# Selective scan beside a feed-forward layer: a quarter of the scan's input reaches the state partitions by DMA in fp32 instead of through TensorE and ScalarE

## The chip, the cores and the metric

The kernel runs on one core of one Trainium2 chip. The metric is the time of one execution on the device in microseconds (us), the median of several runs. TensorE multiplies matrices into PSUM, VectorE and ScalarE work elementwise on SBUF and PSUM, GpSimd works elementwise on SBUF alone, and SyncE issues the DMAs. In the profile they are PE (PEld is its weight load), DVE, ACT, POOL and SP (SPq for what SyncE's queue issues and waits for).

## The reference

Four sublayers follow each other over 2048 tokens of 512 features: linear attention, a feed-forward layer with a Hadamard transform, a selective scan, and a second feed-forward layer. After each comes a residual and a layer norm. The scan is what the change touches:

```python
x = _layernorm(x + _L0_attn_ref(x, ...), axis=-1)
x = _layernorm(x + _L0_ffn_ref(x, ...), axis=-1)
x = _layernorm(x + _L1_attn_ref(x, ...), axis=-1)      # the selective scan
x = _layernorm(x + _L1_ffn_ref(x, ...), axis=-1)

def step(h, inp):                                      # 512 tokens, 4 sequences
    delta_t, B_t, C_t, u_t = inp
    dA = jnp.exp(delta_t[:, :, None] * A[None])
    dBu = (delta_t * u_t)[:, :, None] * B_t[:, None, :]
    h = dA * h + dBu
    y_t = jnp.einsum('bdn,bn->bd', h, C_t)
    return (h, y_t)
```

Each of the 512 features has 32 states. delta is a softplus of a low-rank product of x, and u is x.

## The kernel before

The attention comes first, in a phase of its own. The rest is one phase, `trunk_phase`, in which both feed-forward layers and the scan overlap. Features lie on the partitions, tokens on the free axis, in four tiles of 512 tokens.

The order is written out by hand. Each engine's program is a loop over the same ticks, from -24 to 795, and in each tick each engine adds the instructions that its own conditions name. Engines run freely and meet at semaphores alone. Each tick from 0 to about 770 holds six matmuls of a feed-forward layer (two groups of `three_passes`, L84 to L86; gate, up, and down into the PSUM bank `y_or_aux`). VectorE takes what they give: `silu` (L1524), `hidden` (L1530), and `add` (L1536), which adds the down product to x. The same bank `y_or_aux` serves the sums of the layer norms and the products that prepare the scan, in turns counted by `s_bank`.

Scan step s runs in tick 134 + s, for s from 0 to 511. A step treats 4 features with 32 states each, which fill 128 partitions, over the 512 tokens of a tile. Four steps are a quad; the fourth step of a quad (j = 3, `BY_POOL`) has its product with B made by GpSimd. Eight quads (32 steps) are 128 features, numbered o from 0 to 15. A step is made so:

- SyncE loads delta, spread over the state partitions by a broadcast from DRAM, two steps per DMA, into a ring of six (`delta_load`, L1108), six steps ahead.
- ScalarE makes the decay, exp(delta times A), into one of two PSUM slots (`decay`, L1439).
- TensorE spreads delta*x over the state partitions. Its input are three bf16 parts of delta*x, stacked on 96 partitions (`stk`, loaded by `stack_load`, L1099). The matmul `spread_input` (L1288) picks 4 features and writes one of two PSUM slots `uu`.
- VectorE multiplies that slot with B (`inject`, L1566) one tick ahead of the scan of three steps in four. For the fourth, ScalarE copies the slot to SBUF (`copy_input`, L1447, into the single buffer `us`), since GpSimd reads no PSUM here, and GpSimd multiplies (`inject`, L1673, into `dp`).
- VectorE runs the scan instruction itself (`scan`, L1586).
- GpSimd multiplies the states with C (`times_c`, L1682), and once per quad TensorE sums over the states into `scan_y` (`sum_states`, L1297), five ticks later.
- Once every 32 steps VectorE adds the finished sum to x (`leave`, L1595), and the next `scan_y` waits for that.

The slots `uu` are taken in the order that `spread_turn` gives. GpSimd's share is spread two quads early, in the third tick of a quad, between the shares of VectorE. With two slots, each spread waits for the release of the spread two turns before. The shares of VectorE are released by `inject`, the share of GpSimd by ScalarE's copy.

For each o, delta and delta*x are made two to eight ticks apart (`step_size` L1553, `step_input` L1557), delta*x is cut into its three parts by ScalarE and GpSimd, and SyncE stores both to DRAM (`delta_store` L1086, `parts_store` L1091).

## Time and profile before

| what | value |
|---|---|
| median of 3 runs | 2034.74 us (2029.73 to 2044.35) |
| the profiled execution: its time | 2037.56 us |
| its span in the profile | 2035.8 us |
| the scan, from the first scan instruction to the last | 598.6 to 1827.9 us |
| busy over the span: PE / DVE / ACT / POOL | 1820.4 / 1443.7 / 951.8 / 1285.2 us |
| DMA moved | 427.37 MB |

The span runs from the first to the last instruction of the profiled execution; its time is 1.8 us longer. A row of the profile names the line of the kernel, the engine, the operation, and output<-inputs. A number in brackets with an arrow is the time for which the engine stood idle just before, and what ended it. Matmul records overlap: one matmul's row lasts 0.39 us, while the next starts 0.23 us after it. "PEclk" is the share of full speed that TensorE's clock was granted.

### The profile page before, as it was taken

The numbers are of one execution on the slowest core, as the hardware profiler recorded it, in microseconds if no ns is written. First come the engines' busy times: TensorE is split into PE (matmuls) and PEld (weight loads), VectorE is DVE, ScalarE is ACT, GpSimd is POOL, SyncE is SP. The second block draws the span as 40 slices with busy tenths as digits, with TensorE's granted clock in tenths as the row PEclk, the third lists the DMA queues.
The fourth block names the chain that finished last, engine by engine and source line by source line (L and its number), as shares of the span: only waits on it lengthen the run. The fifth ranks groups of instructions, "written<-read, shape, count | busy, mean of one in ns | idle before, by whom it ended". The sixth has DMA issues, their size and how long they took to land. (4 is left out here: it accounts for less than half of the span.)

```text
span 2035.8 us, 27701 instructions
## 1 busy us (share of the span) xinstructions
PE 1820.4 (89%) x9552; PEld 1144.8 (56%) x9552; DVE 1443.7 (71%) x1825; ACT 951.8 (47%) x1591; POOL 1285.2 (63%) x987
## 2 busy tenths in 40 slices
PE   7899897799998999988998898988988898899997
PEld 5566665568655554544554454554554555567784
DVE  3533424243339998898998999799998999993433
ACT  5434252443255555655555455645554545443212
POOL 4444431366129987897877897697977887782110
PEclk9999999999999999999999999999999999999999
DMA  6433322769558875786776775486766676764451
GB/s 227 141 114 115 115 69 72 264 219 333 193 183 290 280 272 204 250 278 209 251 250 204 257 254 215 177 271 214 263 221 229 219 254 208 256 223 170 186 188 61
DMA packets 132925, 427.37 MB, mean 210 GB/s; under 512 B 29200, under 2 KB 35984, under 8 KB 116016
## 3 DMA queue, kind: packets, MB, share of 16 engines
q1 hardware_dynamic: 132784, 425.59, 60.1%
q8 instruction: 76, 1.25, 0.2%
q14 instruction: 65, 0.53, 0.1%
HBM read 356.34 MB, written 69.21 MB: 209 GB/s over the span
## 5 line engine op out<-in xcount | busy, mean ns | idle before, releaser
L1682 POOL TENSOR_TENSOR h_times_c<-h_states,c_rep 128x512 f32<-128x512 f32 x512 | 671.4, 1323 | 197.7 <-PE scan_y L1297 134.1
L1439 ACT ACTIVATE decay<-delta_on_states,a_neg 128x512 f32<-128x512 f32 x512 | 354.3, 693 | 481.5 <-DVE h_states L1586 469.4
L1648 POOL TENSOR_TENSOR h_lo<-silu_in_h_lo,h_hi 128x512 fp32r<-128x512 f32 x128 | 168.1, 1313 | 250.0 <-ACT h_hi L1354 249.3
L1536 DVE TENSOR_TENSOR x<-x,y_or_aux 128x512 f32<-128x512 f32 x256 | 173.8, 679 | 212.8 <-PE y_or_aux L86 212.8
L1288 PE MATMUL du_spread<-stack,selectors 96*128 96x512 bf16 x512 | 201.2, 393 | 95.6 <-DVE d_b L1566 75.5
L1566 DVE TENSOR_TENSOR d_b<-du_spread,b_rep 128x512 f32<-128x512 f32 x384 | 255.3, 665 | 3.6 <-PE du_spread L1288 3.6
L84 PE MATMUL y_or_aux<-h_hi,w 128*128 128x512 f32 x512 | 239.5, 468 | 15.9 <-ACT b_rep L1404 6.6
L1586 DVE TENSOR_TENSOR_SCAN h_states<-decay,h_last,d_b 128x512 f32<-128x512 f32 x192 | 245.2, 1277 | 9.2 <-ACT decay L1439 4.9
L84 PE MATMUL gate<-x_hi,w 128*128 128x512 f32 x512 | 243.7, 476 | 7.4 <-DVE w L1519 7.1
L84 PE MATMUL up<-x_hi,w 128*128 128x512 f32 x512 | 246.4, 481 | 0.0
L1586 DVE TENSOR_TENSOR_SCAN h_states<-decay,d_b 128x512 f32<-128x512 f32 x192 | 233.6, 1217 | 13.8 <-ACT decay L1439 9.6
L85 PE MATMUL gate<-x_lo,w 128*128 128x512 f32 x512 | 203.2, 397 | 0.0
L85 PE MATMUL up<-x_lo,w 128*128 128x512 f32 x512 | 202.6, 396 | 0.0
L86 PE MATMUL gate<-x_hi,w 128*128 128x512 f32 x512 | 202.5, 395 | 0.0
L86 PE MATMUL up<-x_hi,w 128*128 128x512 f32 x512 | 201.9, 394 | 0.0
L85 PE MATMUL y_or_aux<-h_lo,w 128*128 128x512 f32 x512 | 201.7, 394 | 0.0
L86 PE MATMUL y_or_aux<-h_hi,w 128*128 128x512 f32 x512 | 201.1, 393 | 0.0
L1288 PEld LDWEIGHTS du_spread<-stack,selectors 96*128 96x128 bf16 x512 | 49.5, 97 | 256.4 <-DVE d_b L1566 130.5
L1673 POOL TENSOR_TENSOR d_b_by_pool<-du_copied,b_rep 128x512 f32<-128x512 f32 x128 | 169.6, 1325 | 1.7 <-ACT du_copied L1447 1.7
L1354 ACT CAST h_hi<-silu_in_h_lo 128x512 fp32r<-128x512 f32 x128 | 78.9, 616 | 171.6 <-DVE silu_in_h_lo L1530 171.4
L1530 DVE SCALAR_TENSOR_TENSOR silu_in_h_lo<-silu_in_h_lo,up 128x512 f32<-128x512 f32 x128 | 86.8, 678 | 96.2 <-PE up L86 96.0
L1297 PE MATMUL scan_y<-h_times_c,sum_selectors 128*32 128x512 f32 x1024 | 141.0, 623 | 13.2 <-DVE x L1595 12.8
(167 smaller groups left out, 3142.5 us busy)
## 6 DMA issues: line engine op xcount, KB each, us to landing
delta_on_states<-delta SPq DMA_DIRECT2D x256, 512.0 KB, 5.2
w<-w_split SPq DMA_DIRECT2D x112, 1024.0 KB, 6.7
w<-w_split SPq DMA_DIRECT2D x112, 512.0 KB, 6.3
w_split<-w_presplit_hi_lo SPq DMA_DIRECT2D x32, 512.0 KB, 3.7
w_split<-w SPq DMA_DIRECT2D x16, 1024.0 KB, 6.6
w_presplit_hi_lo<-in_w13b SPq DMA_DIRECT2D x32, 256.0 KB, 3.9
h_times_c<-in_w13a SPq DMA_DIRECT2D x16, 512.0 KB, 4.6
w_split<-w SPq DMA_DIRECT2D x16, 512.0 KB, 6.7
```

What stands on the lines that cost most here:

```text
L84: pe.matmul(out, w_hi, x_hi, start=first, stop=False)
L85: pe.matmul(out, w_hi, x_lo, start=False, stop=False)
L86: return pe.matmul(out, w_lo, x_hi, start=False, stop=last)
L1288: pe.matmul(uu[:, i % NU], sel[:, r, :], stk[:, o % 2, j]).then_inc(s_uu, 1)
L1297: mm = pe.matmul(yb[j * 32:(j + 1) * 32, :], ysel[:, r, :], hc[:, (s + j) % NC_], start=(r == 0), stop=(r == QB - 1), skip_group_check=Tru ...
L1439: act.activation(da[:, s % ND], dring[:, s % NR], ACT.Exp, scale=a[:, column(s):column(s) + 1]).then_inc(s_da, 1)
L1536: dve.tensor_tensor(xt, xt, bank[:, :], ALU.add).then_inc(s_bank, 1)
L1566: dve.tensor_tensor(db[:, by_dve(s) % NB], uu[:, i % NU], brep[:, tile_of(s // SPO) % 2], ALU.mult).then_inc(s_db, 1)
L1586: dve.tensor_tensor_scan(hs[:, s % NH], da[:, s % ND], data, initial, ALU.mult, ALU.add).then_inc(s_hs, 1)
L1648: pool.tensor_tensor(hl[:, idx % 4], sg[:, idx % 4], hh[:, idx % 4].bitcast(F32), ALU.subtract).then_inc(s_hl, 1)
L1673: pool.tensor_tensor(dp[:, quad % 2], us[:, :], brep[:, tile_of(JB * quad // SPO) % 2], ALU.mult).then_inc(s_dp, 1)
L1682: pool.tensor_tensor(hc[:, s % NC_], hs[:, s % NH], crep[:, tile_of(s // SPO) % 2], ALU.mult).then_inc(s_hc, 1)
```

## The change

GpSimd's quarter of delta*x is the last 32 of the 128 features of each o. They leave the path of parts, stack, spread and copy. `delta_x_store` stores them in fp32 to the DRAM tensor `delta_x`, and `delta_x_load` reads them back with a broadcast over the state partitions, one DMA of 256 KB for each quad, into a ring of three (`pring`), from which GpSimd multiplies. The parts shrink from 128 to 96 features. The spreads that are left are numbered by `by_dve`, so that each now waits for VectorE's product two turns before, among the turns of VectorE alone. In other respects the program's order is kept. A buffer of the second layer's weight splitting shrinks from three slots to two, which makes room in SBUF; its instructions stay the same.

```diff
+PD = 32 * BY_POOL
-def spread_turn(s):
-    quad, j = divmod(s, JB)
-    if j == BY_POOL:
-        return JB * quad - 3 if quad else 0
-    return JB * quad + 2 + j - (quad == STEPS // JB - 1)
...
-    parts_d = nc.dram_tensor("delta_x_parts", (NO, P, 3, TT), BF16, kind="Internal").ap()
+    parts_d = nc.dram_tensor("delta_x_parts", (NO, PD, 3, TT), BF16, kind="Internal").ap()
+    du_d = nc.dram_tensor("delta_x", (NO, QD, QB, TT), F32, kind="Internal").ap()
...
-        us = p.sb("du_copied", [P, TT])
+        pring = p.sb("delta_x_on_states", [P, NP, TT])
...
+                def delta_x_store(t, m):
+                    n = KD * t + m
+                    sp.wait_ge(s_du, n + 1)
+                    if n:
+                        sp.wait_ge(s_dx, 16 * n)
+                    sp.dma_start(du_d[n].rearrange("d r t -> r d t"), soft_of(t)[PD:P, m]).then_inc(s_dx, 16)
+
+                def delta_x_load(quad):
+                    o, r = divmod(quad, QB)
+                    if r == 0 or quad < NP:
+                        sp.wait_ge(s_dx, 16 * (o + 1))
+                    if quad >= NP:
+                        sp.wait_ge(s_dp, quad - NP + 1)
+                    sp.dma_start(pring[:, quad % NP], du_d[o, :, r].unsqueeze(0).to_broadcast([NS, QD, TT]))\
+                      .then_inc(s_pr[quad % NP], 16)
...
                     if tick - 2 in PARTS_AT:
                         delta_store(*PARTS_AT[tick - 2])
+                        delta_x_store(*PARTS_AT[tick - 2])
...
+                        for quad in range(NP):
+                            delta_x_load(quad)
+                    if s >= 0 and s % JB == 2 and s // JB + NP + 1 < STEPS // JB:
+                        if s == 2:
+                            delta_x_load(NP)
+                        delta_x_load(s // JB + NP + 1)
...
                 def spread_input(s):
                     o, r, j = place(s)
-                    i = spread_turn(s)
...
-                        if turn == BY_POOL and quad + 3 > STEPS // JB:
-                            pe.wait_ge(s_db, by_dve(JB * quad + JB) + 1)
-                        elif turn == BY_POOL:
-                            pe.wait_ge(s_us, quad + 3)
-                        else:
-                            pe.wait_ge(s_db, by_dve(JB * quad + turn) + 1)
+                    i = by_dve(s)
+                    if i >= NU:
+                        pe.wait_ge(s_db, i - NU + 1)
                     pe.matmul(uu[:, i % NU], sel[:, r, :], stk[:, o % 2, j]).then_inc(s_uu, 1)
...
-                    if s == -1:
-                        spread_input(BY_POOL)
-                        spread_input(JB + BY_POOL)
...
-                    if 0 <= s and s % JB == 2 and s + 2 * JB + 1 < STEPS:
-                        spread_input(s + 2 * JB + 1)
...
-                def copy_input(quad):
-                    i = spread_turn(JB * quad + BY_POOL)
-                    act.wait_ge(s_uu, i + 1)
-                    if quad:
-                        act.wait_ge(s_dp, quad)
-                    act.copy(us[:, :], uu[:, i % NU]).then_inc(s_us, 1)
...
                 def inject(quad):
-                    pool.wait_ge(s_us, quad + 1)
+                    pool.wait_ge(s_pr[quad % NP], 16 * (quad // NP + 1))
...
-                    pool.tensor_tensor(dp[:, quad % 2], us[:, :], brep[:, tile_of(JB * quad // SPO) % 2],
+                    pool.tensor_tensor(dp[:, quad % 2], pring[:, quad % NP], brep[:, tile_of(JB * quad // SPO) % 2],
                                        ALU.mult).then_inc(s_dp, 1)
```

The first place is on TensorE in the quad that ends the 128 features o = 3, near the 908th microsecond of the profile. Before, GpSimd's spread stands between two pieces of the feed-forward layer's up product:

```order
L85 MATMUL up<-x_lo,w 128x512
L86 MATMUL up<-x_hi,w 128x512
L1288 MATMUL du_spread<-stack,selectors 128x512 [waits scan_db]
L84 MATMUL up<-x_hi,w 128x512
L85 MATMUL up<-x_lo,w 128x512
L86 MATMUL up<-x_hi,w 128x512
```

In the changed kernel the two pieces follow each other:

```order
L85 MATMUL up<-x_lo,w 128x512
L86 MATMUL up<-x_hi,w 128x512
L84 MATMUL up<-x_hi,w 128x512
L85 MATMUL up<-x_lo,w 128x512
L86 MATMUL up<-x_hi,w 128x512
```

One spread with its wait went out of each quad, and twelve matmuls of the layer now stand between the spread ahead of this place and the one behind it. The second place is on TensorE a little further on, up to the sum over states that waits for VectorE's `leave` (scan_yout). Before, the last spread ahead of it waits for ScalarE's copy:

```order
L86 MATMUL y_or_aux<-h_hi,w 128x512
L1288 MATMUL du_spread<-stack,selectors 128x512 [waits scan_du_copied]
L84 MATMUL gate<-x_hi,w 128x512 [waits silu_done,w13_in0]
L85 MATMUL gate<-x_lo,w 128x512
L86 MATMUL gate<-x_hi,w 128x512
L1297 MATMUL scan_y<-h_times_c,sum_selectors 32x512 [waits scan_yout,scan_hc]
```

In the changed kernel that wait is for VectorE's product (scan_db):

```order
L86 MATMUL y_or_aux<-h_hi,w 128x512
L1296 MATMUL du_spread<-stack,selectors 128x512 [waits scan_db]
L84 MATMUL gate<-x_hi,w 128x512 [waits silu_done,w13_in0]
L85 MATMUL gate<-x_lo,w 128x512
L86 MATMUL gate<-x_hi,w 128x512
L1305 MATMUL scan_y<-h_times_c,sum_selectors 32x512 [waits scan_yout,scan_hc]
```

Nothing moved here but the wait: the two slots are now turned by VectorE alone. The third place is SyncE's queue at the last store of delta for the second tile, near 905 us. Before:

```order
L1086 DMA delta<-delta_in_x_lo 4x32x512 [waits prep_delta]
L1108 DMA delta_on_states<-delta 128x1x1024 [waits scan_decay] x3
L1065 DMA w<-w_split 128x2048 [waits up_done]
L1091 DMA delta_x_parts<-delta_x_parts_out 128x1536 [waits prep_low]
L1108 DMA delta_on_states<-delta 128x1x1024 [waits scan_decay,delta_stored]
```

In the changed kernel:

```order
L1081 DMA delta<-delta_in_x_lo 4x32x512 [waits prep_delta]
L1088 DMA delta_x<-soft_in_x_hi 8x4x512 [waits delta_x_stored,prep_du]
L1119 DMA delta_on_states<-delta 128x1x1024 [waits scan_decay] x2
L1096 DMA delta_x_on_states<-delta_x 128x1x512 [waits scan_db_by_pool]
L1119 DMA delta_on_states<-delta 128x1x1024 [waits scan_decay]
L1060 DMA w<-w_split 128x2048 [waits up_done]
```

A store that waits for delta*x now stands ahead of the next load of delta, and in every quad a load that waits for GpSimd's product.

## Rows read from the trace of the kernel before

**Rows 1.** Windows: busy us (instructions) of PE, PEld, DVE, ACT, POOL; PEclk, DMA share, GB/s.

```profile
598.60:1827.90 1229.30, 1099.66 (x4829) 627.80 (x4828) 1144.49 (x1346) 656.30 (x1135) 1005.26 (x783) 0.98 0.69 239
```

**Rows 2.** Waits of DVE, 598.6 to 1827.9: us in total, times, longest.

```profile
DVE x L1536 <- PE y_or_aux L86: 33.6, 25, 4.0
DVE silu_in_h_lo L1530 <- PE up L86: 26.5, 19, 5.0
DVE h_states L1586 <- ACT decay L1439: 16.0, 9, 4.2
DVE d_b L1566 <- PE du_spread L1288: 1.4, 2, 1.0
```

**Rows 3.** Waits of PE and ACT in the same stretch.

```profile
PE du_spread L1288 <- DVE d_b L1566: 75.5, 99, 3.0
PE du_spread L1288 <- ACT du_copied L1447: 17.4, 13, 3.6
...
ACT decay L1439 <- DVE h_states L1586: 469.4, 404, 5.2
ACT decay L1439 <- DMA delta_on_states<-delta: 11.4, 5, 4.4
```

**Rows 4.** Timeline of PE and DVE around 917 us (start, duration).

```profile
908.12 0.39 PE L1288 MATMUL du_spread<-stack,selectors 96*128 96x512 bf16 x1 [0.23 <-DVE d_b L1566]
...
912.44 0.39 PE L1288 MATMUL du_spread<-stack,selectors 96*128 96x512 bf16 x1 [0.62 <-DVE d_b L1566]
...
913.83 0.39 PE L86 MATMUL y_or_aux<-h_hi,w 128*128 128x512 f32 x1
914.06 0.39 PE L1288 MATMUL du_spread<-stack,selectors 96*128 96x512 bf16 x1
...
914.53 0.40 PE L85 MATMUL gate<-x_lo,w 128*128 128x512 f32 x1
914.76 0.40 PE L86 MATMUL gate<-x_hi,w 128*128 128x512 f32 x1
...
917.04 0.74 DVE L1595 SCALAR_TENSOR_TENSOR x<-x,scan_feat,scan_y 128x512 f32<-128x512 f32 x1
...
917.93 1.93 PE L1297 MATMUL scan_y<-h_times_c,sum_selectors 128*32 128x512 f32 x8 [2.77 <-DVE x L1595]
```

**Rows 5.** Windows of the tile du_spread: PE, PEld, DVE, ACT busy us (instructions).

```profile
793.00:836.00 43.00, 6.26 (x16) 1.55 (x16) 8.65 (x13) 2.37 (x4) 1.00 0.62 223
1045.00:1080.00 35.00, 5.08 (x13) 1.26 (x13) 7.31 (x11) 1.76 (x3) 1.00 0.60 210
1271.00:1316.00 45.00, 6.25 (x16) 1.55 (x16) 8.65 (x13) 2.37 (x4) 0.96 0.51 188
```

**Rows 6.** Timeline of PE and DVE, 1726 to 1734 us.

```profile
1727.30 0.39 PE L1288 MATMUL du_spread<-stack,selectors 96*128 96x512 bf16 x1 [0.60 <-DVE d_b L1566]
...
1733.44 0.69 DVE L1536 TENSOR_TENSOR x<-x,y_or_aux 128x512 f32<-128x512 f32 x1 [0.69 <-PE y_or_aux L86]
```

**Rows 7.** Timeline of ACT after a softplus (1082 to 1091 us).

```profile
1088.51 0.58 ACT L1447 COPY du_copied<-du_spread 128x512 f32<-128x512 f32 x1
1088.99 0.70 ACT L1439 ACTIVATE decay<-delta_on_states,a_neg 128x512 f32<-128x512 f32 x1
```

**Rows 8.** Timeline at the scan's start (592 to 600 us).

```profile
595.39 0.58 ACT L1447 COPY du_copied<-du_spread 128x512 f32<-128x512 f32 x1 [1.62 <-PE du_spread L1288]
...
597.89 0.70 ACT L1439 ACTIVATE decay<-delta_on_states,a_neg 128x512 f32<-128x512 f32 x1
```

**Rows 9.** Windows of the eleven stretches at half clock within the scan.

```profile
917.30:923.90 6.60, 5.97 (x21) 1.62 (x22) 5.42 (x6) 0.77 (x2) 4.53 (x5) 0.50 0.79 268
...
1777.50:1780.70 3.20, 3.12 (x11) 1.06 (x11) 1.71 (x2) 0.69 (x1) 1.02 (x1) 0.50 0.50 164
sum 45.40, PE 41.38 PEld 19.16 DVE 28.46 ACT 16.87 POOL 22.78; mean PE 3.76 PEld 1.74 DVE 2.59 ACT 1.53 POOL 2.07
```

**Rows 10.** Timeline of PE, 1600 to 1611 us.

```profile
1600.31 0.39 PE L1288 MATMUL du_spread<-stack,selectors 96*128 96x512 bf16 x1 [0.97 <-DVE d_b L1566]
...
1606.51 0.39 PE L1288 MATMUL du_spread<-stack,selectors 96*128 96x512 bf16 x1 [1.59 <-DVE d_b L1566]
```

**Rows 11.** The tile delta_on_states, and SyncE's waits, 598.6 to 1827.9.

```profile
DMA to landing us min/median/max: 3.7/5.2/11.5
...
SPq L1086 <- DVE delta_in_x_lo L1553: 36.1, 13, 4.4
```

56 lines of the change are left out of this document (24 added, 32 removed).

## The prediction

> **What bounds the kernel now.** I read the windows first, by stage. The change acts in the scan alone, 598.6 to 1827.9 us. There DVE is busy 1144 of 1229 us, 93%, and PE 1100 us, 89% [rows 1]. So the two are nearly level, and the order of instructions couples them tick by tick. The waits tell which one sets the pace. DVE, asked whom it waits for, names little: 61.5 us for PE in 46 waits (33.6 + 26.5 + 1.4), and 16.0 us for ACT's decay [rows 2]. PE waits for DVE's products 99 times, 75.5 us, and for ACT's copy of GpSimd's share 13 times, 17.4 us [rows 3]. DVE is thus the bound over most of the scan, and PE becomes it in places. DVE's work is not touched. Whatever PE, ACT or DMA gain can shorten the scan by 61.5 + 16.0 = 77.5 us at most, all DVE idleness there. ACT is far from the bound: of 511 decays 404 wait for the scan before [rows 3].
>
> **The change part by part.**
>
> *One spread fewer per quad on PE, 128 in all.* Its record says 0.39 us, but records overlap; what counts is the distance of starts. With a spread between, L86 to L85 two matmuls on is 913.83 to 914.53, 0.70 us; two ordinary steps are 2 x 0.23 (914.53 to 914.76) [rows 4]. So a spread costs 0.24 us, and 128 of them 31 us of PE work. Most lies where PE would only wait for DVE instead. It counts where DVE waits for PE. I followed PE back from each of DVE's waits to its last idle time over 0.33 us. Three long stretches of unbroken PE work (793 to 836, 1045 to 1080, 1271 to 1316 us) hold 17.9 of the 61.5 us, and 4 + 3 + 4 = 11 spreads for GpSimd, which ACT's count of copies shows [rows 5]: 11 x 0.24 = 2.6 us. The other 30 or so waits end runs of 2 to 15 us, less than two quads, with between none and one such spread each: 0 to 7 us. I counted 13, so 3 us. Together **5.6 us**, with 2.6 and 10 as ends.
>
> *Looser waits of the spreads that stay.* Before, four spreads per quad turned two slots; a spread waited for the product made two ticks before. Now three turn them: the spread for a quad's last step of VectorE still waits for a product of two ticks before, the other two for one of three ticks before. At 912.44 PE idled 0.62 us for a product that it will no longer need [rows 4]. PE gets further ahead, and this is worth something where a short wait of DVE follows closely: 0.69 us at 1733.44 after 0.60 us at 1727.30 [rows 6]. Ten DVE waits of 0.3 to 0.9 us have such a predecessor within 7 us, 5.5 us together. I take **5 us**, ends 0 and 12 (twice as many, if longer waits shrink too).
>
> *128 copies less on ACT.* 0.58 us each, 74 us, hidden under ACT's waiting for the scan [rows 3]. Where the softplus has blocked ACT, the copy stands ahead of the decay that DVE waits for: 1088.51 before 1088.99 [rows 7], 0.5 us, at up to three tiles. At the start of the scan the first decay waits for two copies and a product by GpSimd between them: from 595.39 to 597.89, 2.5 us [rows 8]; about 2 of them fall away, since DVE's first product needs PE's spread, which also comes earlier. Sum **3 us**, ends 1 and 4.
>
> *DMA.* 128 loads of 256 KB are 33.6 MB. The scan's share of 0.69 at 239 GB/s [rows 1] means 346 GB/s when all queues work: 0.76 us a load, 97 us in all, 8 points more of share. Parts and stack shrink by 3 MB, the new stores add 1. Loads of delta land in 5.2 us at the median and 11.5 at worst [rows 11], six steps ahead, and a decay waited for one only five times, 11.4 us [rows 3]. Two things delay them. SyncE's queue is in order: the store of delta*x waits for a product that VectorE makes one tick after the one that the store of delta waits for (already 36.1 us at 13 stores [rows 11]), so the load behind comes some 2.4 us later, 12 times within the scan. And each quad's new load waits for GpSimd's product two quads on; behind it stand the next loads of delta and of weights. In the timeline that product ends ahead of the next delta load's issue in all but 9 of 123 quads. ACT's decays have slack: they wait 1.2 us on average for DVE (469.4 / 404). I take **3 us of loss**, with 0 and 12.
>
> *Clock.* Within the scan the clock was granted at 0.50, the 1.2 GHz level, in eleven stretches, 917.3 the first [rows 9]. DVE was busy in 28.46 of their 45.4 us, so it lost 16.9 us, 1.5 per stretch. The stretch at 917 stands right behind an idle PE: 2.77 us before the sum that waits for VectorE's `leave` [rows 4]. The change makes this idle time longer. From the spread at 908.12 PE needs 0.24 + 12 x 0.23 us to the next spread, 0.24 + 6 x 0.23 to the one after, and 0.24 + 3 x 0.23 to the sum; no product that these wait for comes too late, so it is there at 913.7. Its last matmul ends some 0.2 us later, and it idles until 917.93: 4.0 us against 2.77. Elsewhere waits of one quad that stood apart come together at the one tight spread: 0.97 us at 1600.31 and 1.59 at 1606.51 [rows 10] become 2.56 us in one place. I take four more half-clock stretches at 1.5 us: **6 us of loss**, ends 0 (where the clock falls while PE is ahead, DVE loses nothing) and 20. The Trainium skill, TensorE: Matmul & The Clock Gate, "Why this matters for your kernels", warns against idle gaps between bursts of matmuls, since the clock then falls back to half rate. The trace agrees at 917 us; by that rule this change, which does nothing for PE but make it idle, could give back its gain.
>
> *Nothing else.* GpSimd's product reads SBUF as before; its operand is loaded ten ticks ahead, against 5.2 us for a landing, so that load hides. Were it late, GpSimd and the scan of that step would stand. The parts are cut on 96 instead of 128 partitions; whether that takes three quarters of the time or all of it, it is work of ACT and POOL off the path, and the term is nothing.
>
> Sum: -5.6 - 5 - 3 + 3 + 6 = -4.6 us on the profiled execution's 2037.56, that is 2033.0. That execution is 2.8 us above the median, so the forecast for the median is **2030 us**, 4.6 below 2034.74. With the ends that help, -10 - 12 - 4, it is 2009; with those that hurt, -2.6 - 0 - 1 + 12 + 20, it is 2063.
>
> **The rivals.**
>
> *PE's 31 us come through whole.* If DVE and PE take turns so closely that every delay of PE is passed on, the whole saving counts, 2035 - 31 = 2004, perhaps less the copies that PE waited for. For it: PE is busy 89% of the scan, and VectorE's 77.5 us of waits could hold the gain. Against it: PE had 75.5 us of waiting for DVE left in the same stretch, and the stretches in which DVE waits hold some two dozen of the 128 spreads.
>
> *The slower clock.* Where PE's idle time comes together in one place of each quad, the clock falls far more often. At 1.5 us a stretch, 7 more than before use up what the other terms leave (13.6 - 3 = 10.6 us), and 21 more make the kernel 1% slower, (10.6 + 20.3) / 1.5. If one quad in four brings one, 32 more: 2034.7 + 48 - 10.6, 2072 us. For it: [rows 4, 9, 10]. Against it: nearly all of PE's single waits are below the 2.77 us seen at 917, and with longer lead DVE is covered while PE is slow.
>
> *Loads of delta come late.* The place is SyncE's queue, the price what a late decay costs. The margin: a load needs 5.2 us and has about six steps, some 14 us, less SyncE's own wait. It decides when a landing passes the need, as happened five times. If every eighth of the 256 loads came late by 1.2 us beyond ACT's slack, that is 38 us: 2034.7 - 13.6 + 6 + 38, 2065. For it: landings of up to 11.5 us already and DMA share near 0.8 in some slices, to which 8 points are added. Against it: only 11.4 us of such waits in 511 decays, most of them absorbed by ACT.
>
> **How the numbers follow.** The forecast's own case, a small change with a range of 2018 to 2045, has 0.66; the saving in full 0.14; the clock 0.09; the late loads 0.11. The range from 2009 to 2055 leaves out the whole-saving case's lower half and the far ends of the two slow ones, together below 2 in 10. A measurement of this kernel can tell about 1%, 20 us, from no change (its own runs differ by 15). Faster by more than that: most of the full-saving case and the best end of the forecast's, 0.16. Slower by more: most of both slow cases, 0.15. Within: 0.69.
>
> **What would show it.** In the profile after: DVE still busy about 1144 us in the scan and its waits for PE near 50 us instead of 61.5; PE's busy time down by some 30 us, and its waits for DVE's products up by about as much, in fewer and longer pieces; no wait for a copy; ACT's busy time down by 74 us; DMA bytes up to 459 MB and the scan's share near 0.76; decay waits for DMA from 11 to perhaps 20 us; 13 to 17 stretches at half clock. I would be wrong if DVE's waits for PE fell by half, if PE's clock was granted below 0.96 in the scan, or if decays waited for DMA by more than 30 us.

## The result: slower by 0.7%

The changed kernel takes 2048.73 us (median of 8 runs, 2043.82 to 2054.36), the kernel before on the same chip 2035.57. The ratio is 1.0068, 95% interval 1.0045 to 1.0091. Forecast were 2030 us and a range of 2009 to 2055: the time lies in the range, the sign is wrong. The profiled execution took 2043.82 us (span 2042.0); its scan runs from 593.6 to 1834.2 us, 1240.6 us against 1229.3.

Its window answers to [rows 1] (busy us and instructions of PE, PEld, DVE, ACT, POOL; PEclk, DMA share, GB/s):

```profile
593.60:1834.20 1240.60, 1093.17 (x4707) 639.98 (x4707) 1153.27 (x1346) 592.78 (x1009) 1005.50 (x784) 0.96 0.76 263
```

DVE is busy 8.8 us longer with the same 1346 instructions. ACT lost 64 us, the DMA share is 0.76 as forecast. PE has 122 records fewer but only 6.5 us less busy time: the clock is 0.96 instead of 0.98. The waits of DVE, PE, ACT and SyncE in that stretch answer to [rows 2, 3, 11]:

```profile
DVE x L1529 <- PE y_or_aux L86: 36.9, 26, 3.8
DVE silu_in_h_lo L1523 <- PE up L86: 23.9, 16, 5.2
DVE h_states L1579 <- ACT decay L1444: 15.4, 9, 3.7
DVE d_b L1559 <- PE du_spread L1296: 1.7, 4, 0.8
...
PE du_spread L1296 <- DVE d_b L1559: 73.3, 51, 5.3
...
ACT decay L1444 <- DVE h_states L1579: 497.0, 377, 5.4
ACT decay L1444 <- DMA delta_on_states<-delta: 71.1, 29, 5.1
...
SPq L1096 <- POOL d_b_by_pool L1666: 214.8, 78, 6.5
...
SPq L1088 <- DVE soft_in_x_hi L1550: 30.2, 14, 4.4
```

Three things are to be seen. DVE waits for PE 62.5 us, 61.5 before: no gain from PE's relief shows there. PE's waits for products are half as many (51 for 99) and as long in sum. And ACT's decay waits for a load of delta 29 times, 71.1 us, where it was 5 times and 11.4 us.

Where DVE's 8.8 us are shows when its groups are laid side by side (line, shapes, count | busy us, mean ns | idle before). The kernel before:

```profile
L1542 DVE TENSOR_TENSOR x<-x,mean_or_rank 128x512 f32<-128x512 f32 x32 | 36.5, 1145 | 0.0
L1548 DVE TENSOR_TENSOR x<-x,rstd 128x512 f32<-128x512 f32 x32 | 32.8, 1032 | 0.0
L1553 DVE TENSOR_TENSOR delta_in_x_lo<-delta_in_x_lo,soft_in_x_hi 128x512 f32<-128x512 f32 x15 | 23.2, 1546 | 0.0
L1557 DVE TENSOR_TENSOR soft_in_x_hi<-delta_in_x_lo,x 128x512 f32<-128x512 f32 x15 | 15.2, 1014 | 0.0
```

The changed kernel:

```profile
L1535 DVE TENSOR_TENSOR x<-x,mean_or_rank 128x512 f32<-128x512 f32 x32 | 36.5, 1147 | 0.0
L1541 DVE TENSOR_TENSOR x<-x,rstd 128x512 f32<-128x512 f32 x32 | 34.9, 1095 | 0.0
L1546 DVE TENSOR_TENSOR delta_in_x_lo<-delta_in_x_lo,soft_in_x_hi 128x512 f32<-128x512 f32 x15 | 27.8, 1854 | 0.0
L1550 DVE TENSOR_TENSOR soft_in_x_hi<-delta_in_x_lo,x 128x512 f32<-128x512 f32 x15 | 17.2, 1144 | 0.0
```

These 94 are the only DVE instructions of the scan with both operands in SBUF. Where GpSimd isn't working they last 0.68 us, like their neighbours; beside GpSimd's back-to-back products up to 4.0 in the changed kernel, 4.1 in the kernel before and 4.9 in other kernels of the study. The waiting lies inside the recorded duration, so it counts as busy time and stands in no view of waits. I call **excess** their sum less 94 x 0.685 us: 43.7 before, 52.3 after (over the single records; the rows give it within 0.4). Here is one, in the changed kernel, first DVE's row, then GpSimd's:

```profile
627.33 2.03 DVE L1546 TENSOR_TENSOR delta_in_x_lo<-delta_in_x_lo,soft_in_x_hi 128x512 f32<-128x512 f32 x1
...
626.27 1.30 POOL L1666 TENSOR_TENSOR d_b_by_pool<-delta_x_on_states,b_rep 128x512 f32<-128x512 f32 x1
627.52 2.97 POOL L1675 TENSOR_TENSOR h_times_c<-h_states,c_rep 128x512 f32<-128x512 f32 x2
```

and the same instruction before:

```profile
632.48 0.78 DVE L1553 TENSOR_TENSOR delta_in_x_lo<-delta_in_x_lo,soft_in_x_hi 128x512 f32<-128x512 f32 x1
...
631.41 1.29 POOL L1673 TENSOR_TENSOR d_b_by_pool<-du_copied,b_rep 128x512 f32<-128x512 f32 x1
632.65 2.99 POOL L1682 TENSOR_TENSOR h_times_c<-h_states,c_rep 128x512 f32<-128x512 f32 x2
```

All stand in the same order, alike to 0.04 us. GpSimd's first product ends 0.23 us after DVE's instruction starts. Before, DVE gets its turn then; after, GpSimd's next product does, and DVE waits another 1.25 us. The Trainium skill, SBUF — State Buffer, "SBUF: two separate sides", says of the read and write port that the two engines share that whichever instruction starts first holds it for its whole length and the other blocks. The trace agrees, and shows more: DVE can lose several turns in a row (4.9 us is the end of the running product, three whole ones, and its own time).

The half-clock stretches of the scan, 24 instead of eleven, answer to [rows 9]; two of them and the sum:

```profile
872.30:879.10 6.80, 5.94 (x15) 4.31 (x15) 6.80 (x10) 3.44 (x7) 6.50 (x6) 0.50 0.84 270
...
1554.90:1561.80 6.90, 6.29 (x21) 2.11 (x22) 2.24 (x3) 1.18 (x2) 0.73 (x1) 0.51 0.25 78
...
sum 106.30, PE 97.69 PEld 58.44 DVE 88.46 ACT 49.31 POOL 71.97; mean PE 4.07 PEld 2.43 DVE 3.69 ACT 2.05 POOL 3.00
```

In many DVE stays busy throughout (6.80 of 6.80 us at 872), in some it starves. In all it was idle 106.3 - 88.5 = 17.8 us, against 16.9 in [rows 9]: twice the stretches, and as much idle time of DVE inside them. What PE's slower work costs DVE after a stretch has ended is not in that sum.

### The profile page after: what moved, and what is told of

Its sections match the earlier page's. It is cut to its first block and busy times, and to the rows that moved or that the text cites. A ratio compares the mean times of both kernels' runs of the same rounds, so it can differ in the third digit from the quotient of the medians.

```text
span 2042.0 us, 27348 instructions
## 1 busy us (share of the span) xinstructions
PE 1811.8 (89%) x9424; PEld 1155.3 (57%) x9424; DVE 1452.2 (71%) x1825; ACT 887.0 (43%) x1463; POOL 1283.8 (63%) x987
## 5 line engine op out<-in xcount | busy, mean ns | idle before, releaser
L84 PE MATMUL up<-x_hi,w 128*128 128x512 f32 x512 | 241.5, 472 | 0.0
L1296 PE MATMUL du_spread<-stack,selectors 96*128 96x512 bf16 x384 | 153.6, 400 | 74.4 <-DVE d_b L1559 73.3
L85 PE MATMUL y_or_aux<-h_lo,w 128*128 128x512 f32 x512 | 205.9, 402 | 0.0
L86 PE MATMUL up<-x_hi,w 128*128 128x512 f32 x512 | 202.3, 395 | 0.0
L1666 POOL TENSOR_TENSOR d_b_by_pool<-delta_x_on_states,b_rep 128x512 f32<-128x512 f32 x128 | 171.0, 1336 | 4.3 <-DMA delta_x_on_states<-delta_x 4.3
L84 PEld LDWEIGHTS y_or_aux<-h_hi,w 128*128 128x128 f32 x512 | 100.0, 195 | 96.1 <-issue 29.3
L84 PEld LDWEIGHTS gate<-x_hi,w 128*128 128x128 f32 x512 | 101.7, 199 | 90.5 <-issue 68.8
```

The lines of the kernel that those rows point to most:

```text
L84: pe.matmul(out, w_hi, x_hi, start=first, stop=False)
L85: pe.matmul(out, w_hi, x_lo, start=False, stop=False)
L86: return pe.matmul(out, w_lo, x_hi, start=False, stop=last)
L1296: pe.matmul(uu[:, i % NU], sel[:, r, :], stk[:, o % 2, j]).then_inc(s_uu, 1)
L1666: pool.tensor_tensor(dp[:, quad % 2], pring[:, quad % NP], brep[:, tile_of(JB * quad // SPO) % 2], ALU.mult).then_inc(s_dp, 1)
```

## The experiments

All 18 experiments were timed against the kernel before on the same chip; short_before and short_after, which do less work, are given in the text below. In this table, ratio is to that kernel with its 95% interval, excess, DVE's idle time (gaps over 0.15 us) and half-clock stretches are of the profiled scan, and "late" is what decays waited for loads of delta (us, times).

| kernel | median us | ratio | excess | idle | stretches | late |
|---|---|---|---|---|---|---|
| before | 2034.74 | 1 | 43.7 | 76.2 | 11 | 11.4, 5 |
| before_again | 2033.77 | 0.9999 [0.9984, 1.0015] | 47.4 | 75.1 | 14 | 11.6, 5 |
| null_before | 2034.31 | 0.9996 [0.9981, 1.0012] | 41.6 | 75.6 | 12 | 11.3, 5 |
| before_moved | 2033.27 | 0.9996 [0.9979, 1.0013] | 46.3 | 68.4 | 10 | 16.6, 8 |
| dma96_before | 2034.99 | 0.9999 [0.9981, 1.0018] | 45.2 | 72.9 | 13 | 3.2, 2 |
| before_plus_stores | 2035.94 | 1.0005 [0.9985, 1.0025] | 37.9 | 72.9 | 11 | 16.5, 10 |
| parts96_before | 2039.80 | 1.0030 [1.0015, 1.0045] | 49.4 | 69.0 | 13 | 5.9, 4 |
| before_plus_loads | 2039.72 | 1.0046 [1.0024, 1.0068] | 41.6 | 78.8 | 11 | 74.9, 30 |
| fed_by_dma | 2051.60 | 1.0074 [1.0046, 1.0101] | 54.1 | 77.3 | 13 | 59.7, 25 |
| no_copy | 2049.93 | 1.0057 [1.0037, 1.0078] | 60.9 | 76.7 | 15 | 70.2, 27 |
| tight_waits | 2052.37 | 1.0084 [1.0059, 1.0109] | 58.5 | 77.6 | 17 | 77.8, 27 |
| the change | 2048.73 | 1.0068 [1.0045, 1.0091] | 52.3 | 78.2 | 24 | 71.1, 29 |
| after_moved | 2052.55 | 1.0083 [1.0062, 1.0105] | 54.7 | 83.9 | 30 | 73.9, 27 |
| no_loads | 2046.51 | 1.0071 [1.0051, 1.0091] | 57.0 | 79.1 | 26 | 20.4, 9 |
| double_spread | 2054.41 | 1.0104 [1.0079, 1.0129] | 51.7 | 90.0 | 26 | 82.9, 29 |
| yield_before | 2020.61 | 0.9922 [0.9908, 0.9937] | 25.1 | 80.6 | 12 | 9.8, 6 |
| yield_fed | 2031.42 | 0.9978 [0.9961, 0.9994] | 24.8 | 85.1 | 11 | 52.0, 28 |
| yield_after | 2034.26 | 0.9987 [0.9972, 1.0002] | 26.2 | 94.7 | 24 | 110.7, 41 |

In all of these the scan's length less excess less idle is 1109.0 to 1110.5 us. The rest, DVE's own work, is the same everywhere, so a longer scan shows as one of the two. This is bookkeeping, not a cause: one cause can appear as either. And a profile is one execution only: before_plus_loads was profiled in one of 2037.79 us, beside 2037.56 for the kernel before, and its scan there is 1.4 us longer, though its median is 0.46% above. The ratios carry the argument; the profiles show where to look.

### First: clock, DMA or the looser waits?

**tight_waits**, the changed kernel with two waits as tight as before.

```diff
-                        pe.wait_ge(s_db, i - NU + 1)
+                        pe.wait_ge(s_db, i if s % JB == 0 else i - NU + 1)
...
                         spread_input(s + 1)
+                    if 0 <= s < STEPS and s % JB == 2:
+                        pe.wait_ge(s_db, by_dve(s - 1) + 1)
```

> The changed kernel with the waits of before put back on TensorE, without the matmul and the copy: the first spread of a quad waits for VectorE's product of two ticks before instead of three, and in the third tick of each quad TensorE waits for the product that GpSimd's spread used to wait for. Nothing else is altered. Theory clock (the looser waits gather TensorE's idle time into single long pieces, after which its clock falls to half): the 24 stretches at half clock within the scan fall to 14 or fewer and the time from 2049 to 2035 to 2041 us. Theory DMA (the new loads and their place in SyncE's queue cost the time): 2047 to 2051 us, whatever the clock does. Theory lead (the forecast's term, looser waits are worth 5 us): 2052 to 2056 us.

**no_loads**, the changed kernel without 125 of the 128 loads; GpSimd multiplies the first three rows of delta*x again and again.

```diff
-                    if s >= 0 and s % JB == 2 and s // JB + NP + 1 < STEPS // JB:
-                        ...
-                        delta_x_load(s // JB + NP + 1)
...
-                    pool.wait_ge(s_pr[quad % NP], 16 * (quad // NP + 1))
+                    pool.wait_ge(s_pr[quad % NP], 16)
```

> The changed kernel with the three first loads of delta*x onto the states alone; the other 125 loads of 256 KB and their waits on SyncE are left out, and GpSimd multiplies what stands in its three buffers, so that its quarter of the scan is computed from wrong input. Theory DMA: the time falls from 2049 to 2034 to 2040 us, decays wait for DMA as before the change (11 us). Theory clock: it stays at 2045 to 2050 us with 20 or more stretches at half clock within the scan.

**before_plus_loads**, the kernel before with the change's stores and 124 loads of the same size and place, used by nobody. They all land in one buffer, and to make room for it the edit also takes over the change's smaller buffer of weight splitting, which the expectation doesn't mention:

```diff
-        pre = p.sb("w_presplit", [P, 3, TT])
+        pre = p.sb("w_presplit", [P, 2, TT])
+        spare = p.sb("delta_x_on_states", [P, TT])
...
+                        delta_x_store(*PARTS_AT[tick - 2])
...
+                    if s >= 0 and s % JB == 2 and s // JB + 4 < STEPS // JB:
+                        delta_x_load(s // JB + 4)
```

> The kernel before with the change's DMA traffic added and nothing taken away: one store of 64 KB beside each store of delta, with the wait for delta*x, and one broadcast load of 256 KB per quad (124 in all) at the change's place in SyncE's queue with its wait for GpSimd's product. Nobody reads what is loaded; the store takes delta instead of delta*x. Theory DMA: the time rises from 2036 to 2046 to 2052 us. Theory clock: it stays at 2035 to 2040 us with 9 to 14 stretches at half clock, since TensorE's waits are those of before.

**double_spread**, the changed kernel with each quad's third spread done twice.

```diff
+                    if j == BY_POOL - 1:
+                        pe.matmul(uu[:, i % NU], sel[:, r, :], stk[:, o % 2, j])
                     pe.matmul(uu[:, i % NU], sel[:, r, :], stk[:, o % 2, j]).then_inc(s_uu, 1)
```

> The changed kernel with the third spread of each quad issued twice into the same slot, so that TensorE has as many spreads as before the change (512) and keeps the looser waits; this prices the 31 us of work that the change takes from TensorE. If the forecast's term is right (5.6 us of the 31 count), 2052 to 2057 us against 2049. If TensorE's work counts in full, 2075 to 2080 us. Theory clock: the doubled matmul fills 0.24 us of each quad's idle time, so that some stretches at half clock go and the time may stay at 2047 to 2051 us.

Traffic and smaller buffer together cost the kernel before 0.46%. What the traffic does shows in the waits of ACT and SyncE in before_plus_loads:

```profile
ACT decay L1463 <- DMA delta_on_states<-delta: 74.9, 30, 5.2
...
SPq L1127 <- ACT decay L1463: 371.2, 170, 9.6
SPq L1105 <- POOL d_b_by_pool L1697: 163.9, 71, 5.5
```

and the landings of delta's loads there:

```profile
DMA to landing us min/median/max: 3.6/6.3/13.4
```

SyncE used to stand where it waits for ACT's decay (682.4 us in the kernel before) and issued the load of delta as soon as a buffer was free. Now it stands 71 times behind GpSimd's product first, and the load lands in 6.3 instead of 5.2 us. DVE's waits for the decay are 20.8 us there, 16.0 before, so late decays account for about 5 us in that profile. But no_loads is no faster than the change, though its decays wait only 20.4 us: in the changed kernel the loads cost -0.03%, give or take 0.30. Tight waits give nothing back: waits and clock together (17 half-clock stretches instead of 24) are worth 0.16%, give or take 0.34. The second spread costs 0.36%, give or take 0.34; it brings idle time (90.0), not clock stretches.

### Second: feed, copy, or contended instructions?

**fed_by_dma**, the changed kernel with the fourth spread and ACT's copy of it in their old order and with their old waits, both unread (the ring of loads has two buffers instead of three). **no_copy**, the same without the copy and its waits.

```diff
+                    if 0 <= s and s % JB == 2 and s + 2 * JB + 1 < STEPS:
+                        spread_input(s + 2 * JB + 1)
...
+                    if 0 <= s < STEPS and s % JB == BY_POOL and s // JB + 2 < STEPS // JB:
+                        copy_input(s // JB + 2)
...
                     pool.wait_ge(s_pr[quad % NP], 16 * (quad // NP + 1))
+                    pool.wait_ge(s_us, quad + 1)
```

> The changed kernel with TensorE's fourth spread of each quad and ScalarE's copy of it put back, in the order and with the waits of before; nobody uses the copy, GpSimd multiplies the loaded delta*x (two buffers instead of three) but still waits for the copy as before. It separates GpSimd's feed from what TensorE and ScalarE no longer do. Contention theory (VectorE's 94 instructions with both operands in SBUF wait for GpSimd's, and GpSimd stands in another phase to them once the copy and the spread are gone): as before_plus_loads, 2036 to 2042, ratio 1.000 to 1.004, the excess of the 94 at 40 to 46 us. Clock theory (TensorE's gathered idle time): the idle is not gathered, 11 to 13 half-clock stretches, same time. DMA theory: 2040 to 2046, since all DMA of the change is here. Feed theory (that GpSimd reads another buffer is itself the cause): 2045 to 2050 and an excess above 50 us.

> The changed kernel with TensorE's fourth spread put back (its result unread) but without ScalarE's copy; the spread that follows it in its slot waits for nobody. Beside the run with the copy it shows what the copy's going does, beside the one with before's tight waits and three spreads what the spread's going does. Contention theory: the excess of the 94 instructions jumps where the coupling of GpSimd to the copy goes, so 50 to 58 us here, 2044 to 2051. Clock theory: with the fourth spread TensorE idles less, 11 to 15 stretches and 2036 to 2041. DMA theory: as fed_by_dma. If neither spread nor copy matters by itself the excess is 43 to 50 and the time 2038 to 2044.

This turned the study. With all of PE's and ACT's work back the kernel is as slow as the change, 1.0074, at 13 stretches. From there to the change (no_copy, tight_waits, the change) the ratio moves by -0.17, +0.27 and -0.16%, together -0.06%: what PE and ACT save, less what the clock takes, is nothing within 0.4%. The loss was there before.

That difference of two terms need not be made of two zeros. no_copy and double_spread both have four spreads in each quad, no copy, and the same loads; double_spread has the looser waits and 26 half-clock stretches for 15, and it is 0.47% slower, give or take 0.32 (they differ besides in a buffer of the ring and in the place of the fourth spread). The single executions point the same way. The kernel before was run 29 times on one chip: its mean granted clock went from 0.975 to 0.987, and each 0.001 less goes with 1.3 us more (1.3 to 1.6 on four chips). In the changed kernel, whose median clock is 0.965 for the 0.979 to 0.980 of the kernel before, it is 1.2 us over eight executions. This is a correlation, over whole executions and not the scan alone. So a clock that takes some 10 us and a relief of PE that gives them back are as possible as two terms near nothing; no run separates them.

**short_before** and **short_after**: the 94 instructions, and those of the norms outside the scan, on one column (most of the norms and of delta is left out).

```diff
-                    dve.tensor_tensor(xt, xt, rstd[:, :], ALU.mult).then_inc(s_x, 1)
+                    dve.tensor_tensor(xt[:, :1], xt[:, :1], rstd[:, :1], ALU.mult).then_inc(s_x, 1)
```

> The kernel before, in which VectorE's instructions with both operands in SBUF (step size, step input, and the two of each norm) work on one column instead of 512, everything else in place: most of the norms and of delta and delta*x is left out, so the output is another one. It takes the contended instructions away. By 94 x 0.68 + 43.7 us of excess, less what TensorE then bounds, the scan gets 60 to 105 us shorter, and the norms outside it too: 1880 to 1960 us. What counts is its distance to the same edit of the changed kernel.

> The changed kernel with the same edit (VectorE's instructions with both operands in SBUF work on one column; most of the norms and of delta and delta*x is left out). Contention theory: with the contended instructions gone, so is the loss: short_after minus short_before is between -12 and +4 us, instead of +13. Clock theory: the loss stays or grows, since a less busy VectorE leaves TensorE the bound: +8 to +20. DMA theory: +5 to +13.

They took 1971.98 (ratio 0.9676, 0.9648 to 0.9704) and 1987.98 us (0.9758, 0.9731 to 0.9786): 16 us apart, which only the range given for the clock holds. The edit did not take the contention away, though: one column lasts 0.16 us where GpSimd isn't in the way, and 0.60 and 0.69 us on average (step 303: 0.47 in the one, 1.71 in the other), so these instructions wait for their turn whatever their length. In the profiles the two scans are 19.9 us apart (1180.6 and 1200.5), of which 12.0 are idle time and 8.4 these instructions. So the runs say little on contention, and they don't decide for the clock either.

### Third: does chance decide, and can the contention be removed?

**before_again** is the kernel before. **null_before** has a wait more on GpSimd that never holds.

```diff
                 def inject(quad):
+                    pool.wait_ge(s_lo13, 1)
                     pool.wait_ge(s_us, quad + 1)
```

> The kernel before, unchanged. It shows how much the time, VectorE's waits and the excess of its 94 instructions with both operands in SBUF vary without any edit. Theory that the arbitration between VectorE and GpSimd falls out the same way in each execution of one program: ratio 1.000 within 0.002, excess 42 to 46 us, the same instructions long (step 14 at 0.78 us, 303 at 0.97, 319 at 1.05). If it falls out anew each time: excess 44 to 60 us, other instructions long.

> The kernel before with one wait more on GpSimd ahead of each quad's product, on a semaphore that was reached long before: nothing waits for anything new, only GpSimd's instruction stream is longer by 128 entries. Theory of chance (any edit of GpSimd's stream redraws the arbitration, and the kernel before has a good draw): excess 48 to 60 us and 2040 to 2050 us, as with the change, without any part of the change. Theory that the change's own parts (feed, DMA, clock) cost the time: as the kernel before, 2031 to 2039 us, excess 42 to 46.

My theory that any edit redraws the turns, and that the kernel before has a good draw, fell: both times are the same within 0.16%. Single turns do fall differently (step 319: 1.05, 0.86, 2.33 us; step 122 in the unchanged kernel 1.67 and 2.91), with 41.6 to 47.4 us in sum. A difference of excess of some 4 us between two profiles thus can't be told from chance.

**yield_before** and **yield_after**: GpSimd waits until DVE has done its contended instruction of the tick.

```diff
                     if 0 <= s - 1 < STEPS:
+                        if tick in PARTS_AT:
+                            t, m = PARTS_AT[tick]
+                            pool.wait_ge(s_de, KD * t + m + 1)
+                        ...            (s_du at tick - 1, s_c and s_x of the norms likewise)
                         times_c(s - 1)
```

> The kernel before, in which GpSimd waits, before its product with C in those ticks of the scan where VectorE has an instruction with both operands in SBUF, until that instruction is done. GpSimd can then be at most one instruction ahead in the way. Contention theory: the excess falls from 43.7 us to 10 to 30, and the scan shortens by a half or all of that, 2005 to 2030 us; if GpSimd's own waits come back to VectorE through its products (up to 0.7 us at each), as much is lost: 2035 to 2050.

> The changed kernel with the same waits of GpSimd for VectorE's contended instructions. Contention theory: the excess comes to the same 10 to 30 us as in the kernel before with these waits, and the two times to within 6 us of each other instead of 13, at 2008 to 2035. If the loss of the change lies elsewhere (DMA, clock, waits for TensorE) the two stay 10 to 16 us apart.

Both gain 0.8% (0.9922; 0.9987 / 1.0068 = 0.992), and yield_before at 2020.61 us is the fastest kernel here that does all the work. Its groups:

```profile
L1548 DVE TENSOR_TENSOR x<-x,rstd 128x512 f32<-128x512 f32 x32 | 30.1, 945 | 0.0
L1542 DVE TENSOR_TENSOR x<-x,mean_or_rank 128x512 f32<-128x512 f32 x32 | 28.1, 882 | 0.0
L1553 DVE TENSOR_TENSOR delta_in_x_lo<-delta_in_x_lo,soft_in_x_hi 128x512 f32<-128x512 f32 x15 | 18.2, 1216 | 0.0
L1557 DVE TENSOR_TENSOR soft_in_x_hi<-delta_in_x_lo,x 128x512 f32<-128x512 f32 x15 | 12.8, 854 | 0.0
```

Excess 25.1 instead of 43.7, 18.6 us, of which 4.4 come back as idle time and 13.3 shorten the scan (1216.0). But the two stay 14 us apart at the same excess. The difference stands in idle time now, 94.7 against 80.6. So contention is a cost of both kernels, not the cause of their difference.

### Fourth: addresses, cut parts, and which part of them

**before_moved** and **after_moved** exchange two SBUF tensors in the allocation, so that B and C on the states lie where the other kernel has them.

```diff
-        pre = p.sb("w_presplit", [P, 3, TT])
+        dp = p.sb("d_b_by_pool", [P, 2, TT])
...
-        dp = p.sb("d_b_by_pool", [P, 2, TT])
+        pre = p.sb("w_presplit", [P, 3, TT])
```

> The kernel before, with two SBUF tensors changing places in the allocation (GpSimd's product, 4 KB a partition, where the presplit buffer of 6 KB was, and the reverse), so that B and C on the states lie 2 KB lower as in the changed kernel, VectorE's product and the delta ring 2 KB lower; no instruction differs otherwise. Address theory: the toss at steps 14, 303 and 319 falls as in the changed kernel, excess 48 to 58 us, 2041 to 2050. Otherwise as before, 2032 to 2038, excess 41 to 48.

> The changed kernel, with its ring of loaded delta*x (6 KB) and the presplit buffer (4 KB) changing places in the allocation, so that B and C on the states lie where they did before. Address theory: excess back to 41 to 48 us, 2036 to 2042. Otherwise as the changed kernel: 2046 to 2051, excess 50 to 58.

Addresses do nothing that shows: 0.9996, and 1.0083 against 1.0068, 0.15% with an error of 0.31.

**parts96_before**: the parts made, stored and stacked on 96 partitions. **dma96_before**: made on 128, stored and stacked on 96. In both the fourth spread takes the first step's stack, so GpSimd's quarter is computed from other features.

```diff
-                    act.copy(parts[:, 0], soft_of(t)[:, m]).then_inc(s_p0, 1)
+                    act.copy(parts[:, 0], soft_of(t)[0:PD, m]).then_inc(s_p0, 1)
...
-                    rest = soft_of(t)[:, m]
+                    rest = soft_of(t)[0:PD, m]
```

> The kernel before, with the bf16 parts made, stored and stacked on 96 instead of 128 partitions, as the change does; the fourth spread takes the stack of the first step instead of its own, so a quarter of delta*x is wrong in it. Nothing else of the change is in it. Theory that the cut parts shift GpSimd against VectorE (its two instructions, or the stack's landing): excess 48 to 56 us, 2041 to 2050. Otherwise as before: 2032 to 2038.

> The kernel before, with ScalarE and GpSimd making the parts on all 128 partitions as before, but only 96 stored and stacked, and the fourth spread taking the first step's stack (a quarter of delta*x is wrong). Theory that smaller DMAs turn the arbitration: as the run with everything cut, excess 47 to 55 us, ratio 1.002 to 1.005. Theory that the cut instructions do: as before, excess 41 to 48, ratio 0.998 to 1.001.

The cut by itself costs 0.30%, and it isn't the DMAs: with these alone cut the ratio is 0.9999. What is left is the 64 instructions of ACT and GpSimd on 96 partitions. GpSimd's that make the last part take no less time for it (1.165 us at the median before, 1.170 in the changed kernel). In the profile the step-size instructions of DVE have grown:

```profile
L1554 DVE TENSOR_TENSOR delta_in_x_lo<-delta_in_x_lo,soft_in_x_hi 128x512 f32<-128x512 f32 x15 | 27.8, 1855 | 0.0
```

to the 27.8 us of the changed kernel, from 23.2. But they took 25.7 us in before_again, without any edit:

```profile
L1553 DVE TENSOR_TENSOR delta_in_x_lo<-delta_in_x_lo,soft_in_x_hi 128x512 f32<-128x512 f32 x15 | 25.7, 1712 | 0.0
```

And the profiled scan of parts96_before, 1227.8 us, is no longer than that of the kernel before. So the 0.30% is measured on the medians, and by what route it comes is not shown.

**before_plus_stores**: the 16 stores and their waits, without the loads.

```diff
+                        delta_x_store(*PARTS_AT[tick - 2])
```

> The kernel before, with the 16 stores of 96:128 to DRAM and the waits that the change puts on them (SyncE's for VectorE's product ahead of the next load of delta, ScalarE's for the stores ahead of norms), without the 128 loads; what is stored is read by nobody. Theory that the stores in SyncE's queue cost: ratio 1.003 to 1.005 as with stores and loads together, and waits of the decay for delta up from 14.7 to 18 to 21 us. Theory that the 33.5 MB of loads cost: 0.999 to 1.0015.

1.0005, so it isn't the stores in SyncE's queue, and decays wait 16.5 us instead of 74.9. This kernel keeps the buffer of three slots, though. What it lacks beside before_plus_loads is the loads and the smaller buffer, and the 0.41% between them, give or take 0.30, belongs to the two together.

**yield_fed**: fed_by_dma with the yielding waits.

```diff
                     pool.wait_ge(s_pr[quad % NP], 16 * (quad // NP + 1))
+                    pool.wait_ge(s_us, quad + 1)
...
                     if 0 <= s - 1 < STEPS:
+                        if tick in PARTS_AT:
+                            t, m = PARTS_AT[tick]
+                            pool.wait_ge(s_de, KD * t + m + 1)
+                        ...
```

> The changed kernel with the fourth spread and ScalarE's copy put back (unread) and with GpSimd's yielding waits at VectorE's contended instructions. If contention makes up the loss of the fed kernel and the clock the 14 us between the two kernels with yielding waits: excess 22 to 28, 11 to 14 half-clock stretches, 2018 to 2025, as the kernel before with these waits. If the traffic costs 6 us by itself: 2025 to 2029. If something else of the feed costs the time: 2030 to 2038.

It takes 2031.42 us, against yield_before's 2020.61: +0.56%, give or take 0.22, in the range I had given to something else of the feed than traffic and contention. The excess is equal (24.8), and decays wait 52.0 us for delta instead of 9.8. From there to yield_after, PE's and ACT's relief with the clock's 24 stretches for 11, are +0.09%, give or take 0.22.

### What is shown and what isn't

Shown is where the loss arises: the part of the change that feeds GpSimd by DMA holds all of it, 0.74% in fed_by_dma and 0.56% with the yielding waits, and PE's and ACT's relief, with what the clock takes, adds -0.06 and +0.09%. Shown is also that the cut of the parts costs 0.30% (0.15 to 0.45), by a route that isn't known.

The other half is not pinned down. before_plus_loads costs 0.46% (0.24 to 0.68), and 0.46 and 0.30 make the 0.74 of fed_by_dma. If the 0.46% were the loads, the change without them should be at 1.0022; it is at 1.0071, and the 0.49% between has an error of 0.38. There is a second reading, which I did not test. The smaller buffer of the weight splitting is in before_plus_loads and in every kernel made from the change, and not in before_plus_stores or parts96_before. Were the 0.4% its doing and not the loads', then no_loads, with buffer and cut parts, should be near 1.007, as it is. Against it: its 16 products on GpSimd last 1.29 us at the median with either buffer, and ACT and GpSimd wait no longer around them (24.8 us before, 24.0 with the smaller buffer). The run that would decide is the kernel before with the smaller buffer alone. Nor do the runs tell the two effects of a load apart, its place in SyncE's queue and its traffic: none moves it to another place or queue.

## Why the prediction was wrong, step by step

The prediction was 4.6 us faster, the ratio says 14 us slower. Of the 18 to 19 us between, the failed steps hold: 6 for the cut parts, a term that it put at nothing; 6 to 7 for relief and clock, forecast at -7.6 us and measured at -1; and 6 for the feed, where the 3 us of DMA became 9 together with the smaller buffer, which had no term.

- **"DVE is thus the bound", "DVE's work is not touched".** The first agrees with every kernel: DVE is busy over 91% of each scan. The second was the blind spot: its instructions weren't touched, its busy time was, 1153.3 us instead of "about 1144", though 3.7 us of such a difference came between two profiles of the unchanged kernel. The groups with means of 1.0 to 1.5 us beside neighbours at 0.67 stood in the profile before, and I did not ask what makes them long.
- **PE's spreads (-5.6) and looser waits (-5).** Waits of DVE for PE were 62.5, not "near 50". The looser wait did gather the idle time as described (51 waits for 99), but from fed_by_dma to the change all four terms of PE, ACT and clock, -7.6 us by the forecast, come to -1 us, from -8 to +6. The forecast is just inside that interval, and the sum can't be told from nothing. The one term that was priced by itself, the spreads, came out near its 5.6 us: double_spread costs 7 us, from 0 to 14.
- **Copies (-3).** No wait for them is left. The scan began 5.0 us earlier, but 4.6 earlier in a second profile of the unchanged kernel too: not to be told.
- **DMA (+3, 0 to 12).** A failed step, of which the mechanism was seen and the price is open: 0.46%, 9 us (5 to 14), on the kernel before and with the smaller buffer, nothing within 6 us in no_loads. "In the timeline that product ends ahead of the next delta load's issue in all but 9 of 123 quads" did not hold: SyncE waits for that product 78 times, 214.8 us, with loads of delta queued behind. My bound, "if decays waited for DMA by more than 30 us", was passed, at 71.1. The rival of late loads had the place right (SyncE's queue) and 32 late loads (29 came), but charged 38 us; ACT's slack took nearly all: DVE's waits for the decay stayed at 15.4. The store, which the working counted among the delays, costs nothing within 0.2%.
- **Clock (+6, 0 to 20).** The number of stretches was too low: 24, and 13 to 17 were forecast. PE was idle for 3.87 us at 911.72, beside the 4.0 I worked out, but that is luck. It was a spread, not the sum, and it waited because DVE's step-size instruction ahead of it lasted 3.25 us (0.78 before) beside GpSimd:

```profile
904.86 3.25 DVE L1546 TENSOR_TENSOR delta_in_x_lo<-delta_in_x_lo,soft_in_x_hi 128x512 f32<-128x512 f32 x1
...
907.45 0.40 PE L86 MATMUL y_or_aux<-h_hi,w 128*128 128x512 f32 x1
911.72 0.61 PE L1296 MATMUL du_spread<-stack,selectors 96*128 96x512 bf16 x1 [3.87 <-DVE d_b L1559]
```

  The price is open. DVE's idle time in the stretches is 17.8 us instead of 16.9, not 1.5 more with each, but that leaves out what follows them; by no_copy and double_spread above, the clock may have taken some 10 us that PE's relief gave back. With the yielding waits it is 92.3 - 72.1 = 20.2 us in 24 stretches against 47.8 - 31.6 = 16.2 in twelve. The trace agrees with the rule that I set beside it (idle gaps bring the clock down; the Trainium skill, TensorE: Matmul & The Clock Gate, "Why this matters for your kernels"): the longer idle pieces came with 24 stretches instead of eleven.
- **"Whether that takes three quarters of the time or all of it, it is work of ACT and POOL off the path, and the term is nothing."** The failed step that the runs show most plainly: 0.30%, 6 us (3 to 9). The prediction gave no more reason than that these instructions are off the path. They take as long as before, so what they cost is not their own time; what it is stays open.
- **PE's 31 us whole.** Excluded: a spread added to each quad costs 0.36%, some 7 us of the same 31, and at most 14.

## What to carry to other kernels

Where one engine is busy 93% and still the bound, look for its instructions that last longer than others of their shape: here 94 of them held 44 us of waiting that no view of waits shows, and letting the other engine stand back for them was worth 15 us, more than removing 128 matmuls and 128 copies, of which no gain showed. A prefetch that waits for a slow consumer, put ahead of an urgent load in an in-order queue, makes that load late (5 times before, 29 after); whether moving it would have won the time back was not tried. And a ladder of kernels, each with one part of the change, finds where a loss arises: all of it was there with PE's and ACT's work untouched. The ladder is only as good as its rungs, and every side effect of an edit, like the smaller buffer here, needs a rung of its own.

## What the runs showed of the hardware

- A DVE instruction with both operands in SBUF waits while GpSimd works on SBUF, 0.68 us alone and up to 4.9 with three of GpSimd's 1.29 us products let past. If DVE gets in between, GpSimd's next product lasts 1.73 us. On one column it still takes 0.60 us on average, 0.16 alone.
- Who gets the turn at GpSimd's instruction border can differ at one place between programs whose rows agree to 0.04 us. One program without edits varied by 3.7 us of excess between two profiles.
- GpSimd's and ACT's elementwise instructions on 96 partitions take as long as on 128 (GpSimd 1.170 and 1.165 us, ACT 0.617 and 0.618), and the kernel with them is 0.30% slower, by a route not known.
- Some 32 MB of loads that nobody waits for raised the landing of delta's loads from 5.2 to 6.3 us at the median.
- Among executions of one kernel a lower mean granted clock goes with a longer time: 0.001 less with 1.3 us more, over 29 of the kernel before on one chip.
